# A relu mixture-of-experts layer: gates multiplied into the third layer's inputs, experts paired on 128 partitions, products summed in PSUM

## The reference, cut to what matters

```python
# x: [1, nodes, 256]; shared MLP 256-256-128-256; 4 experts 256-128-64-256
h = relu(einsum('baf,efh->ebah', x, eW1) + eb1[:, None, None, :])
h = relu(einsum('ebah,ehg->ebag', h, eW2) + eb2[:, None, None, :])
o = einsum('ebag,ego->ebao', h, eW3) + eb3[:, None, None, :]
all_out = moveaxis(o, 0, -1)
shared = relu(relu(x @ sW1 + sb1) @ sW2 + sb2) @ sW3 + sb3
gates = softmax(x @ gW + gb, axis=-1)
topv, topi = top_k(gates, 2)
topw = softmax(topv, axis=-1)
sel = take_along_axis(all_out, topi[:, :, None, :], axis=-1)
gated = sum(sel * topw[:, :, None, :], axis=-1)
x = x + shared + gated        # applied to layernorm(x)
```

## Time and profile before

| what | us |
|---|---|
| time, median of 3 runs (6995.93 to 6998.61) | 6998.42 |
| time of the profiled execution | 6996.92 |
| its span, from first to last instruction | 6995.3 |
| the last stage: first product to last addition | 6545.46 to 6989.88 |

### The profile page before, as it was taken

One profiled execution on the slowest core, in us unless ns is written; L12 is line 12 of the kernel. 1 busy time (PEld: TensorE's weight loads), 2 busy tenths in 40 slices (PEclk: granted clock), 3 DMA queues, 4 the chain that ended last, 5 costly groups with the idle time before them and its releaser, 6 DMA issues. The chain is left out here.

```text
span 6995.3 us, 90025 instructions
## 1 busy us (share of the span) xinstructions
PE 4522.6 (65%) x17281; PEld 3227.7 (46%) x17282; DVE 3378.3 (48%) x7997; ACT 843.2 (12%) x2045; POOL 3535.6 (51%) x3600
## 2 busy tenths in 40 slices
PE   1455667635566654556662799999904556676799
PEld 0333444423344442334440588888803444455354
DVE  6366666745566665666666211111164444446344
ACT  0200000100000020000001132222200000003121
POOL 3577777477777747777750500000057777750000
PEclk6777788867778886777885899999957777887777
DMA  5433333343333334333323311211153333330000
GB/s 182 129 105 105 104 105 105 99 114 104 104 104 104 105 94 120 104 104 105 105 74 110 110 46 48 72 49 49 46 157 104 103 102 102 102 98 13 18 16 16
DMA packets 322104, 635.92 MB, mean 91 GB/s; under 512 B 71856, under 2 KB 202344, under 8 KB 320232
## 3 DMA queue, kind: packets, MB, share of 16 engines
q0 software_dynamic: 175472, 478.82, 24.7%
q1 hardware_dynamic: 137016, 148.86, 6.7%
q10 hardware_dynamic: 9552, 7.61, 0.4%
HBM read 537.66 MB, written 97.76 MB: 91 GB/s over the span
## 5 line engine op out<-in xcount | busy, mean ns | idle before, releaser
L941 POOL DMA_INDIRECT rows<-table,ix x2352 | 2299.9, 978 | 741.2 <-issue 686.3
L1201 PE MATMUL acc<-rows,hot 128*128 x5856 | 1624.8, 435 | 229.8 <-DVE hot L1048 174.5
L1201 PEld LDWEIGHTS acc<-rows,hot 128*128 128x128 f32 x5856 | 1164.9, 212 | 645.9 <-issue 436.0
L1246 POOL DMA_INDIRECT rows<-emb,ix x784 | 763.0, 973 | 260.7 <-issue 227.2
L1048 DVE TENSOR_TENSOR hot<-iota,drel 128x256 f32<-128x256 f32 x1464 | 617.9, 428 | 571.5 <-PE acc L1201 568.3
L1367 PE MATMUL acc<-rows,hot 128*128 x1952 | 588.4, 464 | 335.8 <-DVE hot L1288 319.7
L1042 DVE TENSOR_TENSOR rows<-rows,pw 128x1024 f32<-128x1024 f32 x588 | 712.9, 1212 | 0.0
L1367 PEld LDWEIGHTS acc<-rows,hot 128*128 128x128 f32 x1952 | 433.9, 234 | 473.6 <-issue 397.2
L1939 PE MATMUL p<-w,xT 128*128 128x256 f32 x2496 | 556.8, 381 | 22.0 <-ACT xT L1959 22.0
L1930 PE MATMUL p<-xt,w 128*128 128x256 f32 x2496 | 554.5, 380 | 7.5 <-DMA b<-in_b2all 7.5
L1939 PEld LDWEIGHTS p<-w,xT 128*128 128x128 f32 x2496 | 467.8, 190 | 97.2 <-issue 36.8
(11 more groups left out here) (390 smaller groups left out, 4550.0 us busy)
## 6 DMA issues: line engine op xcount, KB each, us to landing
rows<-table,ix POOLq DMA_INDIRECT x2352, 2.8
xg<-slots_in SPq DMA_DIRECT2D x79, 256.0 KB, 2.7
slots_out<-ys SPq DMA_DIRECT2D x78, 256.0 KB
table<-hs SPq DMA_DIRECT2D x147, 130.0 KB, 2.0
own_row<-table SPq DMA_DIRECT2D x21, 896.0 KB, 11.0
slots_in<-zsp SPq DMA_DIRECT2D x9, 1664.0 KB, 22.6
xin<-in_x POOLq DMA_DIRECT2D x14, 896.0 KB, 5.5
rows<-emb,ix POOLq DMA_INDIRECT x784, 2.8
```

The costliest lines, as they stand in the source:

```text
L941: pool.indirect_dma_start(rows[:, h * GB + k, 0:RW], None, table, bass.IndirectOffsetOnAxis(ap=ix[:, h, k:k + 1], axis=0)).then_inc(landed ...
L1201: ins = nc.tensor.matmul(A, hot[j][:, k, :], four[:, j * 2 + k, :], start=False, stop=False, skip_group_check=True)
L1246: pool.indirect_dma_start(rows[:, h * GB + k, 0:D], None, table, bass.IndirectOffsetOnAxis(ap=ix[:, h, k:k + 1], axis=0)).then_inc(landed[ ...
```

## The change

Only `experts_relu` changes, and `program` declares one more array in DRAM, `c.gates`, of 196 rows of 128.

- The gate of a node is multiplied into the expert's hidden vector `g2` ahead of the third layer instead of into the product behind it. For that the gates must lie along the row, the same on all 64 partitions of an expert. PE turns `gate` at the start (two transposes), ACT copies it out (`gate_t`), SP writes it to `c.gates`, waits, and for each block reads it back with four transfers, each of which repeats 7 rows of 512 bytes over 64 partitions, into one of two buffers `wide`. The transfers for block i + 2 are issued when block i has used its own.
- Experts are paired: `g2` holds two experts on 128 partitions, twice. `ew2` is widened with zeros (a memset on DVE ahead of the loads), so that the second layers of a pair are summed into one bank, and ACT evicts two pairs instead of four experts: 9 evictions in a half instead of 11.
- Third layers of a tile are summed in PSUM: three products (shared, pair, pair) into one bank.
- DVE adds the biases apart: to each tile of `X` first `sb3`, then four times gate times `eb3`, each step waiting for the one before (`biased`). Then come four multiplications of `g2` with `wide` (128 by 448 each), then one addition of the finished bank per tile.
- The loops of DVE and SP over blocks are written out instead of run as loops.
- The prologue has 15 loads instead of 12, since pairs are loaded by halves; the first waits for the memset.

```diff
-        UPS = 2 * (6 + 5)
-        NL = 12
+        UPS = 2 * (6 + 3)
+        NL = 15
...
             def _(sp):
+                sp.wait_ge(emptied, 1)
...
+                for o in range(2):
+                    sp.dma_start(eb2[o * 64:o * 64 + 64, :], a["L1_ffn_eb2"][:, o:E1:2], allow_slow_non_contiguous=True
+                                 ).then_inc(loaded, 16)
+                sp.wait_ge(flat, 2)
+                for k in range(2):
+                    sp.dma_start(c.gates[k * P:k * P + gate_t[k].shape[0], :], gate_t[k][:, :]).then_inc(gates_out, 16)
+                sp.wait_ge(gates_out, 32)
+                per_head = c.gates.rearrange("(t k o) q -> o k t q", k=2, o=2)
+
+                def gates(i):
+                    for o in range(2):
+                        for k in range(2):
+                            sp.dma_start(wide[i % 2][o * 64:o * 64 + 64, k, :, :],
+                                         per_head[o:o + 1, k, i * UT:(i + 1) * UT, :].to_broadcast([64, UT, P])
+                                         ).then_inc(spread[i % 2], 16)
+                for i in range(2):
+                    gates(i)
+                for i in range(NB):
+                    if i < NB - 2:
+                        sp.wait_ge(gated, (i + 1) * 4)
+                        gates(i + 2)
+                    sp.wait_ge(added, (i + 1) * UT + 1)
...
-                        for e in range(E1):
-                            pb = bank(m * 11 + 7 + e)
-                            nc.tensor.matmul(pb[0:64, 0:CH], ew2[:, e, :], h1[:, 2 + e, cols],
-                                             start=True, stop=True).then_inc(up, 1)
+                        for e in range(2):
+                            pb = bank(m * 9 + 7 + e)
+                            for k in range(2):
+                                ins = nc.tensor.matmul(pb[:, 0:CH], ew2[:, e * 2 + k, :], h1[:, 2 + e * 2 + k, cols],
+                                                       start=(k == 0), stop=(k == 1))
+                            ins.then_inc(up, 1)
                     for t in range(UT):
-                        pe.wait_ge(bent, o + (12 if (t + 1) * P <= CH else 23))
-                        for e in range(5):
-                            j = t * 5 + e
-                            pe.wait_ge(tmp_made, i * (5 * UT) + (1 + max(j - 3, 0)))
-                            lhs = h2[:, t * P:(t + 1) * P] if e == 0 else g2[:, e - 1, t * P:(t + 1) * P]
-                            rhs = sw3[:, :] if e == 0 else ew3[:, e - 1, :]
-                            nc.tensor.matmul(p3[j % 4][:, 0:D], lhs, rhs, start=True, stop=True).then_inc(down, 1)
+                        pe.wait_ge(gated, i * 4 + (2 if (t + 1) * P <= CH else 4))
+
+                        pe.wait_ge(added, i * UT + (1 + max(t - 3, 0)))
+                        pe.sem_inc(passed[0], 1)
+                        of = slice(t * P, (t + 1) * P)
+                        nc.tensor.matmul(p3[t % 4][:, 0:D], h2[:, of], sw3[:, :], start=True, stop=False)
+                        for e in range(2):
+                            ins = nc.tensor.matmul(p3[t % 4][:, 0:D], g2[:, e, of], ew3[:, e, :],
+                                                   start=False, stop=(e == 1))
+                        ins.then_inc(down, 1)
...
+                v.memset(ew2[:, :, :], 0.0).then_inc(emptied, 1)
...
+                for i in range(NB):
+                    for t in range(i * UT, (i + 1) * UT):
+                        for e in range(5):
+                            if e == 0:
+                                ins = v.tensor_tensor(X[:, t, :], X[:, t, :], sb3[:, :], ALU.add)
+                            else:
+                                dve.wait_ge(biased, t * 5 + e)
+                                ins = v.scalar_tensor_tensor(out=X[:, t, :], in0=eb3[:, e - 1, :],
+                                                             scalar=gate[:, t, e - 1:e], in1=X[:, t, :],
+                                                             op0=ALU.mult, op1=ALU.add)
+                            ins.then_inc(biased, 1)
+                    for m in range(2):
+                        for e in range(2):
+                            dve.wait_ge(bent, i * UPS + (1 + m * 9 + 8 + e))
+                            dve.wait_ge(spread[i % 2], (i // 2 + 1) * 64)
+                            part = g2[:, e, m * CH:(m + 1) * CH]
+                            scales = wide[i % 2][:, e, :, :].rearrange("p t q -> p (t q)")
+                            v.tensor_tensor(part, part, scales[:, m * CH:(m + 1) * CH], ALU.mult).then_inc(gated, 1)
                     for t in range(UT):
+                        n = i * UT + t
+                        dve.wait_ge(down, n + 2)
+                        dve.wait_ge(biased, n * 5 + 5)
+                        v.tensor_tensor(X[:, n, :], X[:, n, :], p3[t % 4][:, 0:D], ALU.add).then_inc(added, 1)
```

More of the change, by code:

```diff
@@ L2080, in experts_relu @@
         sw1, sw2, sw3 = sb("sw1", [P, 2, D]), sb("sw2", [P, 2, P]), sb("sw3", [P, D])
-        ew1, ew2, ew3 = sb("ew1", [P, E1, 2, P]), sb("ew2", [P, E1, 64]), sb("ew3", [64, E1, D])
+        ew1, ew2, ew3 = sb("ew1", [P, E1, 2, P]), sb("ew2", [P, E1, P]), sb("ew3", [P, 2, D])
         sb1, sb2, sb3 = sb("sb1", [P, 2]), sb("sb2", [P, 1]), sb("sb3", [P, D])
-        eb1, eb2, eb3 = sb("eb1", [P, E1]), sb("eb2", [64, E1]), sb("eb3", [P, E1, D])
+        eb1, eb2, eb3 = sb("eb1", [P, E1]), sb("eb2", [P, 2]), sb("eb3", [P, E1, D])
         h1 = sb("h1", [P, 6, UT * P])
         h2 = sb("h2", [P, UT * P])
-        g2 = sb("g2", [64, E1, UT * P])
-        tmp = sb("tmp", [P, 5, D])
+        g2 = sb("g2", [P, 2, UT * P])
+        wide = [sb(f"wide{b}", [P, 2, UT, P]) for b in range(2)]
+        gate_t = [sb(f"gate_t{k}", [n, P]) for k, n in enumerate((P, NT * E1 - P))]
         p1 = [ps(f"p1{k}", [P, 512]) for k in range(4)]
         p3 = [ps(f"p3{k}", [P, 512]) for k in range(4)]
-        loaded, up, bent, down, tmp_made, added, stored = (sem(x) for x in (
-            "loaded", "up", "bent", "down", "tmpm", "added", "stored"))
-        UPS = 2 * (6 + 5)
-        NL = 12
+        loaded, up, bent, down, added, stored = (sem(x) for x in (
+            "loaded", "up", "bent", "down", "added", "stored"))
+        emptied, turned, flat, gates_out, gated, biased = (sem(x) for x in (
+            "emptied", "turned", "flat", "gates_out", "gated", "biased"))
+        spread = [sem(f"spread{b}") for b in range(2)]
+        passed = [sem(f"passed{k}") for k in range(3)]
+        UPS = 2 * (6 + 3)
+        NL = 15
         with nc.Block() as block:
@@ L2112, in _ @@
                     sp.dma_start(to, fr).then_inc(loaded, 16)
[L2113 to L2116, removed]
+                for o in range(2):
[19 more added lines that the diff above has]
+                    sp.wait_ge(added, (i + 1) * UT + 1)
+                    sp.dma_start(out[i * UT * P:(i + 1) * UT * P, :].rearrange("(k p) d -> p k d", p=P),
+                                 X[:, i * UT:(i + 1) * UT, :]).then_inc(stored, 16)
                 sp.wait_ge(stored, 16 * NB)
@@ L2120, in _ @@
             def _(pe):
+                flat_gate = gate[:, :, :].rearrange("p t e -> p (t e)")
+                for k in range(2):
+                    n = gate_t[k].shape[0]
+                    ins = nc.tensor.transpose(p3[k][0:n, 0:P], flat_gate[:, k * P:k * P + n], c.ident[:, :])
+                ins.then_inc(turned, 1)
                 pe.wait_ge(loaded, NL * 16)
@@ L2130, in _ @@
                         for f in range(6):
-                            pb = bank(m * 11 + f)
+                            pb = bank(m * 9 + f)
                             for k in range(2):
@@ L2160, in _ @@
                 with act.Fori(0, NB) as i:
-                    act.wait_ge(down, i * (5 * UT) + 1)
+                    act.wait_ge(down, i * UT + 1)
                     for m in range(2):
                         cols = slice(m * CH, (m + 1) * CH)
-                        for j in range(11):
-                            u = m * 11 + j
+                        for j in range(9):
+                            u = m * 9 + j
                             act.wait_ge(up, i * UPS + (u + 1))
@@ L2180, in _ @@
                 v = nc.vector
+                v.memset(ew2[:, :, :], 0.0).then_inc(emptied, 1)
+                dve.sem_inc(added, 1)
                 dve.wait_ge(loaded, NL * 16)
-                dve.sem_inc(tmp_made, 1)
-                with dve.Fori(0, NB) as i:
-                    for t in range(UT):
[L2185 to L2202, removed]
@@ L2232, in program @@
     c.pass_d = dram("pass_d", [NG, 2, HB])
+    c.gates = dram("gates", [NT * E1, P])
     slots_in, slots_out = (dram(n, [(MAXG + 1) * GS, D]) for n in ("slots_in", "slots_out"))
```

19 lines of the change are left out of this document (13 added, 6 removed).

## The result

The changed kernel takes 6824.41 us (median of 4 runs, 6822.71 to 6831.76), beside it the kernel before 6998.51: a ratio of 0.975 with a 95% interval of 0.9738 to 0.9762, 174 us less. The forecast was 6830, with a range of 6822 to 6852. The profiled execution took 6824.6 us, with a span of 6823.0. It went from 444.42 to 270.43 us.

The account below looks back on a forecast made before the run. Before, PE bounds the up part and DVE the down part; after, PE everywhere. 6552.50 + 210.00 (up) + 63.2 (down) + 0.7 (last addition) + 1.9 (prologue) + 0.6 (end) = 6828.9 profiled; median 1.50 above, so 6830, range 6822 to 6852 us.

Parts of the forecast that it names:

- What bounds the kernel, before and after: Last stage: PE bounds the up part and DVE the down part before (31.09 and 31.53 us); PE everywhere after.
- Up part: PE's half of each block: 14.86 us per half as before, 16.82 for the first, 210.00 us in all.
- the turns of the blocks: Allowance at either end of the range for what seven block turns may win or lose: 4 to 5 us.
- Down part: Third layers: 42 matmuls at 0.215 us, priced from `experts_gelu`, 9.03 us per block, 63.2 us in all.
- the bound of 13.7 us: Down part: upper bound for per-tile waits, 49 x 0.28 us; taken as nothing in the forecast itself.
- DVE's cover: Bias chain of 2.42 us per tile, 16.9 per block, runs under the block's own up part of 29.72 us.
- The decision point: Bias chain plus two multiplications must end in about 29 us; limit 0.79 us per step, 0.48 expected on average.
- Prologue and end: Loads and tail: first product 1.9 us later, 0.6 us for clearing ten more semaphores at the end.
- A: Down part still runs at a low clock: 18.1 us per block, 63 us more, 6894; chance 0.06.
- the 63 us: Extra time if every new down part ran at 1.2 GHz: 7 x 9.03 us.
- B: DVE stays the bound: PE waits 6.3 us per block for the bias chain, 44 us in all, 6874; chance 0.04.
- C: Repeated gate reads run on one DMA engine: 73 us per block at 41 ns per packet, 7082, slower; chance 0.03.

Follow-up runs that it names:

- e3: Kernel before with only the biases added apart, DVE taking each product from PSUM into X in one step instead of two; 6892.29 us.
- e5: Kernel after without the bias chain, sb3 and eb3 left out of the result; 6825.7 us.
- e4: Kernel after, the shared second layer and each pair waiting only for the two evictions they read; 6811.62 us.
- e1: Kernel before with the experts' second-layer weights widened from 64 to 128 columns with zeros; 6995.49 us.
- e9: Kernel after with every read of gates issued twice, once into a buffer nobody uses; 6827.2 us.
- e2: Kernel after without the pairing: each expert alone on 64 partitions, five products per tile; 6892.73 us.
- e6: Kernel after with the bias chain doubled, the second time on a scratch tile; 6891.15 us.
- e10: Kernel after with each read of gates over 64 partitions cut into one over 61 and one over 3; 6862.85 us.

## Why the prediction was right, point by point

**What bounds the kernel, before and after.** Right. Before, DVE in the down part: with two steps made one (e3) the same products took 18.13 instead of 31.53 us, most of it at PE's own pace. After, PE everywhere: e5 (no chain) changed nothing, and e4 (no break on PE) gave all of the break back.

**Up part.** 210.00 us were forecast, 17.74 + 13 x 14.52 = 206.5 came. Two errors partly cancel. "The pairing only lets two share a bank" was wrong: it also removes two changes of form per half, 0.34 us, 4.8 us in all (e1). The sign stood in the rows of before (L2145's group takes 3.15 us for eight matmuls that should take 3.0, rows 2), and I read it as the normal pace. Against that, the first half was taken over as 16.82 us, without the 0.34, and took 17.74, 1.3 us more than those terms give; in two variants that begin in the same way it took 16.27 (e5) and 16.37 (e9), so this is how the clock rose in that execution. The missed 4.8 us stood in no bound of the range. That the time still lies within it, 2.4 us above its lower end, is owed to the 4 to 5 us that were added for another reason, the turns of the blocks: a piece of luck.

**Down part.** 9.03 us forecast, 9.06 came. The price from `experts_gelu` held, and the per-tile waits cost nothing; the bound of 13.7 us for them was far too wide. Summing in PSUM alone would not have done it: e2 shows that the changes to 64 rows and back make a tile slower than the count of matmuls says.

**DVE's cover.** Right, from the written-out chain in `combine`: 2.42 us per tile, and after shows 6603.43 - 6601.02 = 2.41. The decision point was close: with the chain doubled PE waited 8.34 us, where the account written down for that run gave 7.2.

**Prologue and end.** 1.9 us forecast, 14.21 - 13.10 = 1.11 came, from the last gate step to the first product (0.3 to 0.8 in e4, e5, e6, e9 and e10). The way to the first load grew by 0.70 (0.6 forecast), the issues by 1.49 (1.3), but the last landing shrank from 4.54 to 3.46 us, 1.08, since the last loads are small ones; I had bounded that at 0.5. The tail grew from 5.42 to 5.79 us, 0.37 for the ten semaphores (0.6).

**The sum.** Beside the forecast, -3.5 us in the up part, +0.2 in the down part, -0.2 between there and the last addition, -0.8 and -0.2 in prologue and tail, +0.2 for a `router` that ended later make -4.3: 6828.9 were forecast for the profiled execution, and 6824.6 came.

**The rivals.** A (low clock in the down part) didn't come: 1.00. e6 prices a milder case: after a wait of 8.3 us a down part took 1.8 us longer, not twice as long, which is 12 us for 7 of them; a clock that stays low through whole down parts, on which the 63 us rest, came in no run. B (DVE stays the bound) didn't come. C (one DMA engine) didn't come either, and where e10 brought it about it cost 38 us and did not end on the slower side: by the 25 ns per packet of e10 a block's 1792 packets take 45 us, less than the 63.5 us of an old block. So the chance of 0.03 for slower stood on a mechanism that, at this price, could not have given it.

## What to carry to other kernels

When two engines take turns, move the work of the one that follows to where the other is the bound, and read from a written-out chain elsewhere in the same trace what it will cost there; here that alone was worth 106 of 174 us. Before counting matmuls, look at their forms: a change between 128 and 64 rows or columns cost about 0.2 us each time, and half-width products gained only where two could lie side by side. And look at what remains in the chain: a wait for more evictions than the product reads cost more than the bare break in the chain, 0.99 us where it shows 0.72.

## What the runs showed of the hardware that was not expected

- A change of the matmul's form between 128 x 128 and 64 columns or 64 rows took about 0.20 us per change (0.63 instead of 0.43 us for two, 1.92 instead of 1.72 for eight).
- Float32 matmuls of 64 columns on the lower and upper 64 partitions of one bank ran side by side: 1.66 us for eight instead of 3.0.
- Reads of gates cut into 61 and 3 partitions ran at 22 GB/s, 25 ns for a packet of 512 bytes, and eight issues took SP 42.7 us. On 16 engines, in the kernel after, such a packet took 32 ns.
- Four dependent scaled DVE steps took 2.25 us with products from PSUM and two semaphores to wait for, and 2.05 with biases from SBUF and one; a step lasts 0.48 us in both.
